# One PSUM bank for all eight splits of a token block, one output-bias pass per block, and another order of the transfers in the loop's first iteration

## The reference

```
z = einsum('nd,sdr->nsr', layernorm(h), P)         # 8 splits s of 16 values r
scores = einsum('nsr,smr->nsm', z, C)              # 64 experts m in each split
topv, topi = top_k(scores, 4);  w = softmax(topv)
h1 = gelu(einsum('nsr,nskrh->nskh', z, W1[s, topi]) + b1[s, topi])   # 32 hidden values
yl = einsum('nskh,nskhr->nskr', h1, W2[s, topi]) + b2[s, topi]
comb = einsum('nskr,nsk->nsr', yl, w).reshape(n, 128)
out = gelu(comb @ G1 + g1b) @ G2 + g2b             # 128 -> 64 -> 192, added to h
```

## Time and profile before

| | |
|---|---|
| median of 3 runs | 876.96 us (875.22 to 881.2) |
| the profiled execution | 874.15 us, span 872.3 us |
| TensorE busy | 838.7 us, 96% of the span |
| ScalarE busy | 597.0 us, 68% |
| VectorE busy | 658.1 us, 75% |
| GpSimd busy | 531.9 us, 61% |
| DMA | 154.41 MB, mean 177 GB/s |
| first layer L914 | 768 rows, 209.5 us busy |
| second layer L978 | 1536 rows, 203.9 us busy |
| spread transfers | 192 of 512 KB, median 5.5 us from issue to landing |

### The profile page before, as it was taken

One profiled execution on the slowest core, in us unless ns is written; L12 is line 12 of the kernel. 1 busy time (PEld: TensorE's weight loads), 2 busy tenths in 40 slices (PEclk: granted clock), 3 DMA queues, 4 the chain that ended last, 5 costly groups with the idle time before them and its releaser, 6 DMA issues.

```text
span 872.3 us, 16321 instructions
## 1 busy us (share of the span) xinstructions
PE 838.7 (96%) x5438; PEld 393.4 (45%) x5438; DVE 658.1 (75%) x1613; ACT 597.0 (68%) x906; POOL 531.9 (61%) x483
## 2 busy tenths in 40 slices
PE   9999999999999988899999999999999999999997
PEld 5777778777778765222222222222222223222222
DVE  5576666666575898788788887788778887876774
ACT  2452324334442476889897989798979897987884
POOL 0556476546365736666865686659566866676553
PEclk8999999999999999999999999999999999999999
DMA  9700011000001099998878897888688888898773
GB/s 242 268 2 1 2 40 39 1 1 1 2 1 22 10 168 201 296 281 243 275 229 269 250 275 226 260 260 278 203 277 250 271 265 252 255 274 285 256 246 104
DMA packets 90260, 154.41 MB, mean 177 GB/s; under 512 B 30345, under 2 KB 56521, under 8 KB 89788
## 3 DMA queue, kind: packets, MB, share of 16 engines
q1 hardware_dynamic: 90178, 153.38, 59.6%
HBM read 139.09 MB, written 15.83 MB: 178 GB/s over the span
## 4 chain that ended last, share of the span: by engine, by line
PE 77%; ACT 10%; DVE 4%; issue 4%; DMA 2%; POOL 1%; SPq 0%; DVEq 0%; POOLq 0%; ACTq 0%
PE ps L978 18%; PE ps L914 17%; PE ps L954 5%; PE ps L533 5%; PE ps L560 4%; PE ps L663 3%; PE ps L541 3%; DMA wbc<-w_rows 2%; PE ps L574 2%; PE ps L742 2%; PE ps L623 2%; ACT ring L1339 2%; PE ps L647 2%; PE ps L763 1%; ACT L1214 1%
## 5 line engine op out<-in xcount | busy, mean ns | idle before, releaser
L2092 POOL TENSOR_TENSOR ring<-ring,wbc 128x512 f32<-128x512 f32 x192 | 245.7, 1282 | 139.9 <-ACT ring L1348 122.6
L1857 DVE TENSOR_TENSOR ring<-ps,ring 128x1024 f32<-128x1024 f32 x192 | 234.6, 1222 | 70.5 <-PE ps L954 49.5
L914 PE MATMUL ps<-zst,w1st 99*128 99x512 bf16 x768 | 209.5, 382 | 16.3 <-ACT ring L1339 10.1
L978 PE MATMUL ps<-ring,w2cur 128*32 128x512 f32 x1536 | 203.9, 604 | 0.0
L1339 ACT ACTIVATE ring<-ps 128x1024 f32<-128x1024 f32 x192 | 196.7, 1025 | 5.5 <-PE ps L914 5.4
L1350 ACT ACTIVATE ps<-ps 128x512 f32<-128x512 f32 x192 | 113.0, 588 | 55.2 <-PE ps L914 54.9
L1860 DVE TENSOR_TENSOR ring<-ps,wbc 128x512 f32<-128x512 f32 x192 | 130.7, 681 | 3.8 <-DMA wbc<-w_rows 3.7
L914 PEld LDWEIGHTS ps<-zst,w1st 99*128 99x128 bf16 x768 | 60.7, 97 | 136.3 <-issue 34.5
L1348 ACT ACTIVATE ring<-ps 128x512 f32<-128x512 f32 x192 | 116.4, 606 | 0.0
L1931 POOL TENSOR_TENSOR s2q<-s2q,rope 128x768 f32<-128x768 f32 x24 | 43.1, 1819 | 82.6 <-ACT s2q L1128 82.6
L954 PEld LDWEIGHTS ps<-wst,sel 32*128 32x128 bf16 x384 | 18.0, 90 | 148.4 <-DVE ring L1857 94.4
(11 more groups left out here) (201 smaller groups left out, 1284.8 us busy)
## 6 DMA issues: line engine op xcount, KB each, us to landing
wbc<-w_rows SPq DMA_DIRECT2D x192, 512.0 KB, 5.5
w2cur<-in_w SPq DMA_DIRECT2D x48, 256.0 KB, 4.7
zst<-z_parts SPq DMA_DIRECT2D x72, 64.0 KB, 4.7
w_parts<-wp SPq DMA_DIRECT2D x69, 64.0 KB, 3.2
w1st<-w_parts SPq DMA_DIRECT2D x12, 256.0 KB
wst<-w_parts SPq DMA_DIRECT2D x24, 128.0 KB, 4.0
z_parts<-zp SPq DMA_DIRECT2D x6, 384.0 KB, 5.7
wst<-w_parts SPq DMA_DIRECT2D x24, 96.0 KB, 3.9
```

Of the source, the lines that this page charges most:

```text
L914: return pe.matmul(bank(to), w1st[0:99, 4 * a + j, col:col + P], zst[0:99, (i // 2) % 2, j, :], start=True, stop=True)
L978: mm = pe.matmul(bank(YBANK, 0, 512, 32 * j, 32 * j + 32), w2cur[:, n, j, :], ring[:, (4 * g + j) % RING, :], start=False, stop=(n == 7 an ...
L1857: dve.tensor_tensor(v, ps[:, WBANK * 512:WBANK * 512 + 1024], v, ALU.mult).then_inc(s["duo_done"], 1)
L2092: pool.tensor_tensor(ring[:, slot, :], ring[:, slot, :], wbc[:, g % 4, 1, :], ALU.mult).then_inc(s["tri_done"], 1)
```

## The change

It has two parts.

**One bank for a block.** The second-layer weights of half a are put into columns 16a to 16a+15 of the 32 of their split place, with zeros in the others. So the two halves of a block write disjoint rows of the same bank, and the bank keeps summing over all four iterations of the block. The bias is then added once per block, in 4 matmuls over 128 gate rows; for this the scores' weights `cblk` are reordered so that gate rows of a tile come as (j; a, expert), and `b2w` holds both halves. `keep_y` and its waits happen once per block, `first_final` has 2 matmuls instead of 4, `ysum` is used in two places. The gate parts and rows that are stored and loaded change their addresses with it: `store_rows` writes all 128 partitions of one row group in each of its two transfers. `g1` and `b2w` are half as large, and their places are kept free.

**Iteration 0.** `load_w1(sp, 1)` moves from ahead of the loop to the end of the group n = 7 of iteration 0; `store_z(1)` and `store_z(2)` move from n = 1, 2 to n = 3, 4; the first `load_z` of the loop moves from n = 3 to n = 6.

The diff, without the allocations and parts of the host's layouts:

```diff
@@ -319,7 +321,7 @@
                 sp.dma_start(dst, src).then_inc(s["ld_mid"], 16)
             sp.dma_start(w1f[:, :], t["w1"]).then_inc(s["ld_w1"], 16)
             sp.dma_start(b1f[:, :], t["b1"]).then_inc(s["ld_w1"], 16)
-            sp.dma_start(w_parts[:, :, :, :, :, 3, :].rearrange("a j t r m n -> (a j t r m) n").bitcast(F32),
+            sp.dma_start(w_parts[:, :, :, :, :, 3, :].rearrange("j a t r m n -> (j a t r m) n").bitcast(F32),
                          t["zeros"].to_broadcast([S * M // 2, B * T // 2])).then_inc(s["zeroed"], 16)
             sp.wait_ge(s["w1_lo"], 1)
             for k in range(3):
@@ -337,14 +339,14 @@
                 sp.wait_ge(s["wT_done"], tile + 1)
                 blk, col = divmod(tile, 4)
                 for jj in range(2):
-                    sp.dma_start(w_rows[:, :, blk, jj, col * P:col * P + P].rearrange("a m n -> m a n"),
-                                 gates_of(tile)[M * jj:M * jj + M, 1:4:2, :]).then_inc(s["r_stored"], 16)
+                    sp.dma_start(w_rows[:, :, blk, jj, col * P:col * P + P].rearrange("a m n -> (a m) n"),
+                                 gates_of(tile)[:, 2 + jj, :]).then_inc(s["r_stored"], 16)
 
             def store_gates(tile):
 
                 sp.wait_ge(s["lo_done"], LENT + tile + 1)
                 for k in range(3):
-                    sp.dma_start(w_parts[:, :, :, :, :, k, tile * P:tile * P + P].rearrange("g j t r m n -> (j t r m) g n"),
+                    sp.dma_start(w_parts[:, :, :, :, :, k, tile * P:tile * P + P].rearrange("j a t r m n -> (a t r m) j n"),
                                  wp_of(tile)[:, k, :, :]).then_inc(s["w_stored"], 16)
 
             def load_z(m):
@@ -365,7 +367,7 @@
                 sp.wait_ge(s["w_stored"], 48 * min(TILES, 4 * blk + 4))
                 if i >= 2:
                     sp.wait_ge(s["duo_w"], 8 * (i - 1))
-                v = [w_parts[a, j, kt, :, :, :, blk * BLK:blk * BLK + BLK].rearrange("r m k n -> (r m k) n") for j in range(2)]
+                v = [w_parts[j, a, kt, :, :, :, blk * BLK:blk * BLK + BLK].rearrange("r m k n -> (r m k) n") for j in range(2)]
                 sp.dma_start(wst[:, i % 2, 0, :], v[0]).then_inc(s["wst_ld"], 16)
                 sp.dma_start(wst[32:P, i % 2, 1, :], v[1][0:96, :]).then_inc(s["wst_ld"], 16)
                 sp.dma_start(wst[0:32, i % 2, 1, :], v[1][96:P, :]).then_inc(s["wst_ld"], 16)
@@ -433,9 +435,8 @@
             load_gates(0)
             spread(2)
             spread(3)
-            load_w1(sp, 1)
             load_ones(1)
-            finals = ((g1[:, :, :], t["g1"]), (g1b[0:GH, 0:1], t["g1b"]), (g1b[GH:P, 0:1], t["g1b"]),
+            finals = ((g1[:, :], t["g1"]), (g1b[0:GH, 0:1], t["g1b"]), (g1b[GH:P, 0:1], t["g1b"]),
                       (g2[0:GH, :], t["g2"][0:GH, :]), (g2[GH:P, :], t["g2"][0:GH, :]))
             for g in range(GROUPS):
                 i, n = divmod(g, 8)
@@ -448,12 +449,14 @@
                     load_gates(i + 1)
                 if n == 4 and i + 1 < NIT and (i + 1) % 4 == 0:
                     load_gates(i + 1)
-                if n == 3 and i % 2 == 0 and i + 2 < NIT:
+                if n == (3 if i else 6) and i % 2 == 0 and i + 2 < NIT:
                     load_z(i // 2 + 1)
                 if n == 5 and i % 4 == 1 and i > 1:
                     store_out(i // 4 - 1)
-                if n in (1, 2) and i == 0:
-                    store_z(n)
+                if n in (3, 4) and i == 0:
+                    store_z(n - 2)
+                if n == 7 and i == 0:
+                    load_w1(sp, 1)
                 if n >= 3 and i == 1:
                     dst, src = finals[n - 3]
                     sp.dma_start(dst, src).then_inc(s["ld_final"], 16)
@@ -962,34 +965,33 @@
                     pe.wait_ge(s["w2_lo"], 16 * (i + 1))
                 if n == 4:
                     pe.wait_ge(s["w2_hi"], 16 * (i + 1))
-                if n == 0 and kt == 0:
+                if n == 0 and kt == 0 and a == 0:
 
                     pe.wait_ge(s["wT_done"], 4 * blk + 4)
-                    if g > 0:
-                        pe.wait_ge(s["y_kept"], g // 16)
+                    if blk > 0:
+                        pe.wait_ge(s["y_kept"], blk)
                     rows = wT_odd if blk % 2 else wT_even
                     for j in range(4):
-                        pe.matmul(bank(YBANK, 0, 512, 32 * j, 32 * j + 32), b2w[:, 4 * a + j, :],
-                                  rows[:, 2 * a + j // 2, :], start=True, stop=False, skip_group_check=True)
+                        pe.matmul(bank(YBANK, 0, 512, 32 * j, 32 * j + 32), b2w[:, j, :],
+                                  rows[:, j, :], start=True, stop=False, skip_group_check=True)
                 pe.wait_ge(s["duo_done"], g + 1)
                 pe.wait_ge(s["two_done"], g + 1)
                 pe.wait_ge(s["tri_done"], g + 1)
                 for j in range(4):
                     mm = pe.matmul(bank(YBANK, 0, 512, 32 * j, 32 * j + 32), w2cur[:, n, j, :],
                                    ring[:, (4 * g + j) % RING, :],
-                                   start=False, stop=(n == 7 and kt == 1), skip_group_check=True)
+                                   start=False, stop=(n == 7 and kt == 1 and a == 1), skip_group_check=True)
                 mm.then_inc(s["second_done"], 1)
 
             def first_final(blk, to):
 
                 if blk == 0:
                     pe.wait_ge(s["ld_final"], 16 * 5)
-                pe.wait_ge(s["y_kept"], 2 * blk + 2)
-                for a in range(2):
-                    for half in range(2):
-                        mm = pe.matmul(bank(to, 0, 2 * P, GH * half, GH * half + GH), g1[:, a, :],
-                                       ysum[:, (2 * blk + a) % 4, half * 2 * P:half * 2 * P + 2 * P],
-                                       start=(a == 0), stop=(a == 1), skip_group_check=True)
+                pe.wait_ge(s["y_kept"], blk + 1)
+                for half in range(2):
+                    mm = pe.matmul(bank(to, 0, 2 * P, GH * half, GH * half + GH), g1[:, :],
+                                   ysum[:, blk % 2, half * 2 * P:half * 2 * P + 2 * P],
+                                   start=True, stop=True, skip_group_check=True)
                 mm.then_inc(s["u_full"], 1)
 
             def second_final(blk, half, to):
@@ -1314,12 +1316,12 @@
             copy_scores(LEAD, PBANK)
             z_mid(2)
 
-            def keep_y(m):
-
-                act.wait_ge(s["second_done"], 16 * m + 16)
-                if m >= 4:
-                    act.wait_ge(s["u_full"], m // 2 - 1)
-                act.copy(ysum[:, m % 4, :], bank(YBANK)).then_inc(s["y_kept"], 1)
+            def keep_y(blk):
+
+                act.wait_ge(s["second_done"], 32 * blk + 32)
+                if blk >= 2:
+                    act.wait_ge(s["u_full"], blk - 1)
+                act.copy(ysum[:, blk % 2, :], bank(YBANK)).then_inc(s["y_kept"], 1)
 
             def final_gelu(blk, at):
 
@@ -1342,8 +1344,8 @@
                     keep_gates(tile - 1, PBANK)
                 if i % 2 == 1 and n == 0 and tile <= TILES:
                     keep_gates(tile - 1, PBANK)
-                if g >= 18 and g % 16 == 2:
-                    keep_y(g // 16 - 1)
+                if i % 4 == 0 and i > 0 and n == 2:
+                    keep_y(i // 4 - 1)
                 act.wait_ge(s["tri_full"], g + 1)
                 act.activation(ring[:, slot + 3, :], bank(TBANK), ACT.Gelu_apprx_tanh).then_inc(s["tri_gelu"], 1)
                 act.wait_ge(s["two_full"], g + 1)
@@ -1991,9 +1993,9 @@
                 pool.wait_ge(s["wT_done"], tile + 1)
                 if tile > 0 and tile != 3:
                     pool.wait_ge(s["w_stored"], 48 * before(tile))
-                pool.tensor_copy(wp_of(tile)[:, 0, :, :], gates_of(tile)[:, 0:4:2, :]).then_inc(s["hi_done"], 1)
+                pool.tensor_copy(wp_of(tile)[:, 0, :, :], gates_of(tile)[:, 0:2, :]).then_inc(s["hi_done"], 1)
                 pool.wait_ge(s["hi_done"], tile + 1)
-                pool.tensor_tensor(wr[:, :, :], gates_of(tile)[:, 0:4:2, :], wp_of(tile)[:, 0, :, :], ALU.subtract).then_inc(s["r_done"], 1)
+                pool.tensor_tensor(wr[:, :, :], gates_of(tile)[:, 0:2, :], wp_of(tile)[:, 0, :, :], ALU.subtract).then_inc(s["r_done"], 1)
 
             def low_parts(tile):
                 pool.wait_ge(s["r_done"], tile + 1)
@@ -2179,26 +2181,27 @@
     for b in range(B):
         wblk[CIN * b:CIN * b + CIN, D * b:D * b + D] = g["L0_tok_proj_w"].T
         wblk[B * CIN, D * b:D * b + D] = g["L0_tok_proj_b"]
-    cblk = np.zeros((S, R, S, M), f)
+    cblk = np.zeros((S, R, 4, 2, M), f)
     for k in range(S):
-        cblk[k, :, k, :] = g["L0_ffn_C"][k].T
+        cblk[k, :, k % 4, k // 4, :] = g["L0_ffn_C"][k].T
     w2 = np.zeros((2, 2, 8, 4, P, 32), f)
     for k in range(S):
         v = g["L0_ffn_W2"][k].reshape(2, 8, 4, HID, R)
         if k % 4 >= 2:
             v = v.transpose(0, 1, 3, 2, 4)
```

(11 more changed lines are left out.)

10 lines of the change are left out of this document (6 added, 4 removed).

## The result

The changed kernel takes 881.37 us (median of 14 runs, 878.52 to 885.49), the kernel before 876.32 us (14 runs on the same chip). The ratio is 1.0058, 95% interval [1.0040, 1.0075]: 0.6% slower. The profiled execution took 881.05 us, span 879.3 us, 7.0 us more than the span before.

The account below looks back on a forecast made before the run. TensorE was taken to bound plain groups, ScalarE the exponentials, and spread transfers iteration 0. Removed work -4.5 and moved transfers +6 gave +1.5 on the 876.96 us median: 878.5 us, range 867 to 886.

Parts of the forecast that it names:

- rival 3's cheap form: TensorE's clock falls in the group 11 wait, 7 us at half speed: up to 3.5 us, 882 us; rival 3's chance 0.22.
- Removed work: Bias passes, ScalarE copies and halved output-layer matmuls, each priced at its place in the chain of waits: -4.5 us.
- Rival 2: The removed work was on the path everywhere: -12.5 + 6, 870.5 us; chance 0.15.
- Won at groups 4 to 8: Iteration 0: spreads 4 to 7 no longer stand behind the weights, so group 8 ends 2.9 us earlier, at 363.1.
- The wait at group 11: Iteration 0: spread 11, queued behind the moved weights, is issued about 365 and lands 377.2; a wait of 8.5 us.
- 120 to 150 GB/s: Sign to look for: the DMA rate from about 361 us, during the wait near 368 to 378.
- Rival 1: The weights hide and spread 11 lands before 368.7, so no wait at group 11: 868.9 us; chance 0.13.
- Pacing of groups 12 to 14 by transfers: Iteration 0: spreads 12 to 14 come about 3 us apart instead of 2.29, costing another 1 us.
- The expensive form: Rival 3 with the clock low until group 19, eight groups: +11 us, 889 us; rival 3's chance 0.22.
- Where the loss was to stay: Iteration 0's moved transfers: +6 us at group 19's exponential, bounds -2 and +9, not given back afterwards.
- the stop of rows 5: A small stop before the transfer landing at 389.3, near group 18, absorbed in the shift: some 0.7 us given back.
- Stores of gate rows, constants: Rearranged row stores of the same bytes and two smaller constants: 0, bounds -0.5 and +0.5 us.

Follow-up runs that it names:

- e9: The changed kernel with the removed half of the output-bias passes issued again at the second half of each block; 877.22 us, one profiled execution.
- e1: The changed kernel with iteration 0's transfers back in the old order, only the one-bank part left; 872.75 us, ratio 0.9957 to the kernel before.
- e4: The changed kernel with the z stores and z loads back at their old places, weights still after group 7; 879.54 us, ratio 1.0032 to before.
- e11: The changed kernel with three of the six 256 KB weight transfers ahead of the loop, the rest behind group 7's spread; 876.14 us, ratio 0.9999 to before.
- e5: The changed kernel with nine dummy matmuls on TensorE during the wait for spread 11; 878.75 us, ratio 1.0035 to the kernel before.
- e3: The changed kernel with the second first-layer weight load ahead of the loop again, z transfers in their new places; 871.76 us, ratio 0.9943 to before.
- e6: The changed kernel with six 16-partition weight transfers replaced by one to 96 partitions, same place; 877.47 us, ratio 1.0019 to the kernel before.
- e7: The changed kernel with the weights in one 96-partition transfer and that load ahead of the loop; 868.94 us, ratio 0.9928 to the kernel before.

## Why the forecast came out as it did

The forecast was 878.5 us, within 1%, range 867 to 886; measured 881.37. The sign, the removed work and the wait were right, and the size of the loss was 2.9 us short. The largest part of that is a term that the sum had put at nothing: the clock, 2.4 us. The measured time stands beside rival 3's cheap form, 882 us, to which I had given 0.22, rather than beside the forecast. Against the median of before in the same runs, the forecast's +1.5 stands beside +5.05.

1. **Removed work: -4.5 forecast, -4.1 found.** Output layers 6 x 0.43 instead of 6 x 0.5; group 176 0.97 instead of 1.1; the exponentials 0.14 each instead of 0.1. Reading each removed instruction at its place in the chain held, down to "bias under the table load: nothing" (e9). Rival 2 (all of it on the path, -12.5) is out: e1 measured -3.8 with an interval from -1.8 to -5.8.
2. **Won at groups 4 to 8: 2.9 forecast, 2.5 found.** Group 8's product ended at 362.95 + 0.68 = 363.6, forecast 363.1. In e9, whose transfers are placed alike and whose clock stayed at 1.00 there, the gain is 3.0; the rest is the clock's fall at the loop's start.
3. **The wait at group 11: 8.5 forecast, 8.67 found** (and 1.07 at group 10, not forecast). That these two agree so well is luck, because both ends of the wait came later than forecast. Spread 11 was issued at 366.84, not 365, mostly because SP's issues of weights and z took 4.4 and 3.7 us, not 4.0 and 2.7, and landed 12.24 us later at 379.08, not at 377.2. VectorE was ready for it at 370.5, not 368.7. The queue moved 153 to 195 GB/s from 366 to 375 us, so the sign "120 to 150 GB/s" did not come, and the 122 to 145 taken was too low for this execution, though not for e4 (131 to 149). No run shows the 1.5 us for the signal by itself. Group 11 ended 6.9 us late, counted from group 0, 5.7 forecast. Other executions of the same order waited 7.0 to 9.1 us. Rival 1 (the weights hide) is out; e11 shows that half of them still don't.
4. **Pacing of groups 12 to 14 by transfers: +1 forecast, 0 found.** No spread was waited for there, and with the clock up (e5) the shift does not grow from the end of group 11 to the start of group 13. In its place came **the clock**: groups 12 and 13 at the 1.2 GHz level, +2.4 by the difference between the change and e5. This is the term that the sum had left out. I had it as rival 3, cheap form, and against it that the loop's short gaps had left the clock at 1.00; but this gap is 8.14 us, and in e11 the clock fell in one of 2.71. The row that bore on it was that of 16 to 23 us. A forecast wait of 8.5 us should have carried the clock in the sum: 878.5 + 2.4 = 880.9. The expensive form (eight groups at half speed) did not come, the clock was back within two groups after the wait.
5. **Where the loss was to stay: +6 at group 19 forecast, +8.9 found.** The 2.9 between them are 1.2 from the end of group 11, -1.1 from the pacing, 2.4 from the clock, and 0.4 because the stop of rows 5 gave back 0.3 and not 0.7. It was not given back, as forecast: +8.9 at group 23, and after that the bank change's steps and the one stop at group 158.
6. **Stores of gate rows, constants: 0 forecast.** Nothing in the starts contradicts it; group 0 starts 0.2 us later, within what group 0 varies between the traces (-1.3 to +1.2).

Open: why the wait at group 11 varies from 7.0 to 9.7 us between executions of the same order; and what makes the stops of 1.0 to 2.9 us come in some executions and not in others (a fall of the clock in e1, e3, e6 and e7, a late spread in the change) was seen, not controlled.
